# The first attention of an eight-part network: who scales the probabilities, and how heads of 96 fill tiles of 128

## What is computed

```python
q = (latents @ Wq.T).reshape(b, q_len, H, HD)        # H, HD = 16, 96; latents: layernorm of x
k = (hidden @ Wk.T).reshape(b, s_len, KV, HD)        # KV = 4; hidden: context (64 rows), then latents (256)
v = (hidden @ Wv.T).reshape(b, s_len, KV, HD)
q = q.transpose(0, 2, 1, 3).reshape(b, KV, G, q_len, HD)      # G = 4 heads for one of keys
scores = jnp.einsum('bkgqd,bksd->bkgqs', q, k) * scale        # scale = 96 ** -0.5; 320 keys
attn = jax.nn.softmax(scores.astype(jnp.float32), axis=-1)
out = jnp.einsum('bkgqs,bksd->bkgqd', attn, v)
return out.transpose(...).reshape(b, q_len, H * HD) @ Wo.T
```

## Time and profile before

| | us |
|---|---|
| runs, median (lowest to highest) | 1707.35 (1707.07 to 1708.24) |
| profiled execution, its own time | 1711.2 |
| its span, first to last instruction | 1709.4 |
| mean granted clock of TensorE in it, as a share of 2.4 GHz | 0.893 |

### The profile page before, as it was taken

How to read it: one execution, slowest core, us unless ns; L and a number is a source line. 1 busy time by engine, 2 the same in 40 slices (tenths; PEclk the granted TensorE clock), 3 DMA queues, 4 the chain that set the end, 5 groups by cost and what they waited for, 6 DMA issues and landing times.

```text
span 1709.4 us, 18898 instructions
## 1 busy us (share of the span) xinstructions
PE 1443.9 (84%) x6489; PEld 1131.2 (66%) x6489; DVE 1083.9 (63%) x2489; ACT 458.6 (27%) x994; POOL 296.5 (17%) x170
## 2 busy tenths in 40 slices
PE   6569999998999898899646878858999778789998
PEld 5347776776677667688545767747887546567786
DVE  4556876767777666948886756554446399944142
ACT  3223423332343333313131202101221333322010
POOL 4101111111111111202021002111543121012120
PEclk9779999999999999999855699557999889899999
DMA  5521232322232212222001112200112000001011
GB/s 184 159 77 46 80 82 68 82 74 58 64 89 71 75 50 69 72 66 67 25 26 46 42 40 60 63 18 1 50 49 62 26 25 1 1 27 60 16 36 49
DMA packets 99407, 96.40 MB, mean 56 GB/s; under 512 B 13138, under 2 KB 72418, under 8 KB 99314
## 3 DMA queue, kind: packets, MB, share of 16 engines
q1 hardware_dynamic: 98802, 94.35, 19.0%
q0 software_dynamic: 512, 0.85, 0.2%
HBM read 84.34 MB, written 10.82 MB: 56 GB/s over the span
## 4 chain that ended last, share of the span: by engine, by line
PE 62%; DVE 25%; issue 4%; ACT 4%; DMA 2%; SPq 1%; POOL 1%; DVEq 0%; ACTq 0%; POOLq 0%
PE bank L1636 48%; PE bank L1977 5%; PE bank L1728 4%; DVE nf_y L1581 3%; DVE st L1141 2%; DVE xn L1159 1%; PE bank L1661 1%; DVE xT L1118 1%; PE bank L1718 1%; DVE mx L1192 1%; DVE mx L1498 1%; ACT e L936 1%; DMA nf_w<-in_L_w 1%; DVE sm L1510 1%; SPq L767 1%
## 5 line engine op out<-in xcount | busy, mean ns | idle before, releaser
L1636 PE MATMUL bank<-xT,slots 128*128 128x512 f32 (+1 forms) x1920 | 467.6, 402 | 9.6 <-DVE xT L1118 7.8
L1636 PEld LDWEIGHTS bank<-xT,slots 128*128 128x128 f32 (+1 forms) x1920 | 354.8, 186 | 109.0 <-issue 8.9
L813 POOL TENSOR_TENSOR slots<-staging,slots 128x1024 fp32r<-128x1024 f32 (+4 forms) x97 | 230.5, 2379 | 1103.0 <-ACT slots L903 1103.0
L1581 DVE TENSOR_SCALAR nf_y<-nf_w 128x512 fp32r<-128x512 f32 (+2 forms) x495 | 232.2, 496 | 29.0 <-PE bank L1977 28.0
L1636 PE MATMUL bank<-slots,h 128*128 128x512 f32 (+1 forms) x728 | 178.8, 405 | 20.1 <-DVE h L1248 13.9
L1977 PE MATMUL bank<-nf_y,nf_d 128*128 128x512 f32 (+2 forms) x495 | 170.6, 429 | 10.3 <-DVE nf_y L1581 8.0
L1636 PEld LDWEIGHTS bank<-slots,h 128*128 128x128 f32 (+1 forms) x728 | 140.8, 194 | 56.1 <-DVE h L1248 14.8
L903 ACT ACTIVATE slots<-staging 128x1024 fp32r<-128x1024 f32 (+4 forms) x97 | 98.1, 1018 | 189.9 <-PE bank L1636 174.2
L936 ACT ACTIVATE e<-bank,mx 128x320 f32<-128x320 f32 x128 | 66.4, 523 | 271.1 <-DVE mx L1195 254.0
L1977 PEld LDWEIGHTS bank<-nf_y,nf_d 128*128 128x128 f32 (+1 forms) x495 | 95.3, 197 | 47.0 <-issue 15.5
L1214 DVE TENSOR_TENSOR x<-bank,x 128x512 f32<-128x512 f32 x72 | 49.7, 690 | 110.9 <-PE bank L1636 110.6
(11 more groups left out here) (246 smaller groups left out, 1897.8 us busy)
## 6 DMA issues: line engine op xcount, KB each, us to landing
staging<-in_L_wqkT SPq DMA_DIRECT2D x16, 480.0 KB, 3.8
nf_out<-nf_w SPq DMA_DIRECT2D x30, 256.0 KB, 2.1
staging<-nf_out SPq DMA_DIRECT2D x30, 256.0 KB, 2.8
staging<-in_L_woT SPq DMA_DIRECT2D x16, 384.0 KB, 3.5
staging<-in_L_w SPq DMA_DIRECT2D x12, 512.0 KB, 4.0
nf_a<-nf_max SPq DMA_DIRECT2D x40, 128.0 KB, 3.6
nf_r<-nf_rcp SPq DMA_DIRECT2D x40, 128.0 KB, 3.4
nf_w<-in_L_w SPq DMA_DIRECT2D x15, 256.0 KB, 4.4
```

The costliest lines, as they stand in the source:

```text
L813: g.tensor_tensor(lo, split_source(i), hi.bitcast(FP32), ALU.subtract).then_inc(*sig.mark("weight_low", i))
L1581: v.tensor_scalar(nf_y[0:rows, i % STAIR_RING, 0:size], w_, bound, first, compare, ALU.mult)\
L1636: ins = mm(dst, l_, r_, start=i == 0, stop=i == len(passes) - 1)
```

## The change

It has three parts.

1. **Probabilities.** The reciprocals stay on VectorE; the two multiplications of 128x320 go to ScalarE, as copies with a factor from SBUF for each row. In the list they keep the place of `scale0(n-1)`, so ScalarE does them after the exponentials of unit n and before the copies of `turn0(n-2)`.
2. **The factor of the scores** is multiplied into the queries when they are evicted (both parts), so that the exponential needs no scale and the small multiplication of the maxima goes.
3. **Four heads in three tiles.** The host lays out the query weights of a group as three tiles of 128 columns: 96 of head j and 32 of head 3. `q0` gets 128 partitions. Each of the three products is evicted by two instructions, of 96 and of 32 partitions, the second to the place of head 3 in the fourth plane of `q0`. The output of head 3 is evicted in three pieces of 32 partitions, each to the upper 32 partitions of one of the three planes, so that `o0` multiplies three full tiles of 128 rows, with rows of the output weights in the same order. The chunks of `o0` are then 128 partitions with two tiles and with one.

The planner's cost of a `q0` step goes from 2.6 to 3.5.

```diff
-    steps += [("k0", 0), ("kc0", 0)] + [("q0", 0, h) for h in range(HPG)]
+    steps += [("k0", 0), ("kc0", 0)] + [("q0", 0, j) for j in range(QT0)]
...
-                steps += [("q0", s + 1, h) for h in ((0, 1), (2,), (3,))[j - 5]]
+                steps.append(("q0", s + 1, j - 5))
...
-        q0 = sb("q0", [HD0, 2, 2, HPG, HALF], F32R, s0)
+        q0 = sb("q0", [P, 2, 2, HPG, HALF], F32R, s0)
...
-            for i in range(2):
-                rows = a["L0_woT"][(s % G0 * HPG + 2 * i) * HD0:(s % G0 * HPG + 2 * i + 2) * HD0]
-                chunk(("o0", s, i), HD0, (2, D), [((slice(None),), rows.rearrange("(h p) n -> p h n", p=HD0))])
+            for i, n in enumerate((2, 1)):
+                rows = a["L0_woT"][(s % G0 * QT0 + 2 * i) * P:(s % G0 * QT0 + 2 * i + n) * P]
+                chunk(("o0", s, i), P, (n, D), [((slice(None),), rows.rearrange("(h p) n -> p h n", p=P))])
...
ScalarE:
-            def q0_(s, h):
-                high("q0", (s, h), q0[:, s % 2, 0, h], psum(("q0", s, h))[0:HD0])
+            def q0_(s, j):
+                bank = psum(("q0", s, j))
+                act.wait_ge(*sig.when("q0_product", (s, j)))
+                sc.activation(q0[0:HD0, s % 2, 0, j], bank[0:HD0], ACT.Copy, scale=HD0 ** -0.5)
+                sc.activation(q0[spare(j), s % 2, 0, QT0], bank[HD0:P], ACT.Copy, scale=HD0 ** -0.5).then_inc(*sig.mark("q0_high", (s, j)))
...
+            def scale0(n):
+                act.wait_ge(*sig.when("sums0", n))
+                for i in range(TPB):
+                    e = e0[:, (2 * n + i) % E0_RING]
+                    sc.activation(e, e, ACT.Copy, scale=sm[:, n % 4, 2 + i:3 + i]).then_inc(*sig.mark("probs0", (n, i)))
...
             def pv0(n, s, bl, h):
-                high("pv0", n, q0[:, s % 2, 0, h, bl * S:(bl + 1) * S], psum(("pv0", n))[0:HD0, 0:S])
+                cs, bank = slice(bl * S, (bl + 1) * S), psum(("pv0", n))
+                if h < QT0:
+                    high("pv0", n, q0[0:HD0, s % 2, 0, h, cs], bank[0:HD0, 0:S])
+                    return
+                act.wait_ge(*sig.when("pv0_product", n))
+                for j in range(QT0):
+                    ins = sc.activation(q0[HD0:P, s % 2, 0, j, cs], bank[spare(j), 0:S], ACT.Copy)
+                ins.then_inc(*sig.mark("pv0_high", n))
...
VectorE (its q0_ and pv0 change in the same way: two and three subtractions for one):
             def scores0(n, s, bl, h):
...
-                link(ins)
-                v.tensor_scalar(mx[:, n % 4, 2:4], mx[:, n % 4, 0:2], HD0 ** -0.5, None, ALU.mult)\
-                    .then_inc(*sig.mark("max0", n))
+                ins.then_inc(*sig.mark("max0", n))
 
             def scale0(n):
                 dve.wait_ge(*sig.when("exp0", (n, TPB - 1)))
-                link(v.reciprocal(sm[:, n % 4, 2:4], sm[:, n % 4, 0:2]))
-                for i in range(TPB):
-                    v.tensor_scalar(e0[:, (2 * n + i) % E0_RING], e0[:, (2 * n + i) % E0_RING], sm[:, n % 4, 2 + i:3 + i], None, ALU.mult)\
-                        .then_inc(*sig.mark("probs0", (n, i)))
+                v.reciprocal(sm[:, n % 4, 2:4], sm[:, n % 4, 0:2]).then_inc(*sig.mark("sums0", n))
...
TensorE:
-                qk(s, ("q0_product", (s, h)), h * HD0, (h + 1) * HD0, lambda k: xt(k, hf * HALF, (hf + 1) * HALF), bank[0:HD0])
+                qk(s, ("q0_product", (s, j)), j * P, (j + 1) * P, lambda k: xt(k, hf * HALF, (hf + 1) * HALF), bank[:])
...
-                pe.wait_ge(*sig.when("q0_low", (s, h)))
+                pe.wait_ge(*sig.when("q0_low", (s, min(h, QT0 - 1))))
...
-                pairs = [([q0[:, s % 2, p, h, i * P:(i + 1) * P] for p in range(2)], [w[h // 2][p][:, h % 2] for p in range(2)])
-                         for h in range(HPG)]
+                pairs = [([q0[:, s % 2, p, j, i * P:(i + 1) * P] for p in range(2)], [w[j // 2][p][:, j % 2] for p in range(2)])
+                         for j in range(QT0)]
```

45 lines of the change are left out of this document (32 added, 13 removed).

## The result

The changed kernel takes 1743.84 us (median of 4 runs, 1741.22 to 1747.87) against 1707.80 for the kernel before beside it. The ratio is 1.0212, 95% interval 1.0188 to 1.0237: 36 us slower, where 34 us faster was forecast. The profiled execution of the changed kernel has 1741.5 us.

A forecast was written before the change was run, and what follows sets the result against it. TensorE, 94% busy, was taken to pace the first attention from 130 to 620 us. Profiled 1711.2 - 40.3 + 5 + 1 = 1677 us, so 1673 us for the median of runs; range 1652 to 1697.

The forecast's parts named there:

- +5: First attention's new instruction order: 14 us back at seven stage starts, 9 off for the removed multiplication; bounds -19 and +30.
- the chain stays hidden: Units with a projection: TensorE needs 4.13 + 2.9 us, the ScalarE-VectorE chain 5.0, so the longer chain costs nothing there.
- The 2 us of room: Units with a projection: slack between TensorE's 4.13 + 2.9 us and the chain's 5.0, used as argument against ScalarE's queue.
- 14 for them and for head 3's evictions together: Two bare units at each stage start: longer chain makes TensorE wait 2 us, seven times, 14 us back.
- rival 3: Slower: ScalarE's queue becomes the path, scalings ahead of the turned copies; 64 + 19 less 40 gives +43, 1750 us; chance 0.06.
- -40.3: First attention: removed matmuls worth their 0.24 us spacing; output products 23.0 us, query products of stages 2 to 7 17.3.
- The outputs' 23.0 us: o0 products in the first attention: 8 stages x 12 fewer matmuls x 0.24 us, 23.0 us off.
- The queries' 17.3: q0 products of stages 2 to 7, where TensorE is full: 6 x 12 fewer matmuls x 0.24 us, 17.3 us off.
- The bound of +30: Worst case for the new order: all 3.0 us lost at each stage start, and TensorE's clock lower a while after each.
- a clock under 0.95: Sign of a wrong forecast: TensorE's granted clock in the first attention's stretch below 0.95, against 0.98 before.
- forecast -9: Stage starts: the multiplication between maximum and exponential, held up by GpSimd's splits, falls away; 9 us off.
- The tail: After the last unit, of head 3, o0 waits for three evictions in series instead of one: 1 us more, unhidden.

The follow-up runs named there:

- e5: Kernel before with only the scores' factor moved into the query evictions and the small multiplication of the maxima gone: 1704.82 us, ratio 0.9967.
- e7: Kernel before with the factor in the evictions and only the outputs packed; queries unpacked, scalings on VectorE, query cost 2.6: 1690.59 us, ratio 0.9894.
- e13: e3 with the planner's cost of a query product 10.4/3 for 3.5, so a stage sums as in the kernel before: 1693.14 us, ratio 0.9910.
- e3: Changed kernel with the scaling of the probabilities back on VectorE; factor and packing stay: 1703.31 us, ratio 0.9969.
- e1: Kernel before with only the scaling of the probabilities moved to ScalarE: 1740.01 us, ratio 1.0187.
- e16: e7 with two unused 32x320 copies a unit added on ScalarE at the scalings' place; VectorE keeps its scalings: 1722.49 us, ratio 1.0082.
- e9: e3 with planner's costs that put every step but the fourth query product where the kernel before has it: 1715.42 us, ratio 1.0032.
- e11: e9 without the second evictions of the query tiles from stage 2 on, so head 3 uses old queries: 1690.81 us, ratio 0.9880.
- e10: e7 with two query products a stage evicted twice, on ScalarE and VectorE, and no matmul removed: 1705.58 us, ratio 0.9980.
- e15: e7 without two of head 3's three output evictions from stage 2 on: 1688.47 us, ratio 0.9880.
- e17: Kernel before with the planner's cost of a query product 2.625 for 2.6, so a stage sums to 10.5: 1714.99 us, ratio 1.0043.
- e18: Changed kernel with the planner's cost of a query product 10.4/3 for 3.5: 1737.55 us, ratio 1.0168.

## Why the prediction was wrong

From the kernel before to the changed one in the parts that the runs had, by their ratios times 1708 us: factor -5.6 (e5), packed outputs -12.5 (e7), packed queries with even costs +2.7 (e13, with an interval that takes in 0), the planner's cost +10 (e3), the scalings on ScalarE +41 (changed kernel). The sum is +36, as it has to be for steps in a row; in another order a step is worth something else, as the scalings' 32, 41 and 44 us show. TensorE over the attention, from 56 us on, in us:

| | length | busy | idle | at 1.2 GHz |
|---|---|---|---|---|
| before | 580.6 | 518.6 | 62.0 | 65 |
| changed | 603.9 | 508.4 | 95.4 | 120 |
| e1, scaling alone | 606.2 | 535.9 | 70.3 | 99 |
| e3, scaling back | 564.6 | 489.7 | 74.9 | 92 |
| e7, outputs packed | 558.6 | 495.6 | 63.0 | 58 |
| e13, even costs | 559.0 | 483.6 | 75.3 | 72 |
| e16, two copies added to e7 | 585.9 | 509.3 | 76.6 | 82 |

**Right, with their sizes.** 192 matmuls fewer. The spacing of matmuls with 96 and with 128 rows: twelve took 3.05 us, nine 2.34; less the last one's 0.40 that is 0.241 and 0.243 us. The scaling on ScalarE takes 0.555 us a piece (forecast 0.52) and a pair 1.01. The evictions cost as whole ones, by length and not by partitions:

```profile
L953 ACT ACTIVATE e<-e,sm 128x320 f32<-128x320 f32 x108 | 54.4, 555 | 4.5 <-DVE sm L1226 4.4
...
L937 ACT ACTIVATE q<-bank 96x512 fp32r<-96x512 f32 x20 | 11.9, 593 | 2.9 <-PE bank L1666 2.9
L938 ACT ACTIVATE q<-bank 32x512 fp32r<-32x512 f32 x20 | 11.8, 592 | 0.2
```

The Trainium skill's formula (ScalarE: Activation LUTs) gave 0.546 as an estimate; the trace has 0.555. Its rule to put a multiplication on VectorE was right here. The reason that the runs show lies in the queue, more than in the single instruction (0.555 us against VectorE's 0.384).

**The step that failed first: "+5" for the new order**, with "in the units with a projection beside them (2.9 us more of TensorE) the chain stays hidden". The 2 us of room came from a unit of 5.0 us with *one* background step on VectorE. The trace of before had the real number:

```profile
L1581 DVE TENSOR_SCALAR nf_y<-nf_w 128x512 fp32r<-128x512 f32 x317 | 158.2, 522 | 10.6 <-PE bank L1977 9.9
```

That is 317 steps for the stretch's 57 units, 2.8 us a unit where I had counted 0.42. The list of steps puts 2 or 3 of them into each of the two bare units of a stage, and in most stages 5 to 9 into each of the six others, the very ones with a projection. TensorE's longer work there left VectorE little room: 38.6 us of waits for TensorE in the stretch, 0.7 us a unit in the mean and not 2. That the background steps took the room is argued from these counts; no run took them away. I said of VectorE "neither is the bound by its sum", from busy time alone. So a longer chain counts in far more units than the two bare ones: the scalings cost 32 to 44 us where I had 14 for them and for head 3's evictions together, and e16 gives 32 us for 64 pairs, 0.5 us of each pair's 0.9. That was rival 3's mechanism. Its +43 stands near the result's +36 in part by luck: it took 64 us for the scalings, 19 for head 3 and -40 for the matmuls, where the runs have 32 to 44, 2 to 6 and some -12, and it had nothing for the planner's 10. I gave it 0.06, on the strength of that room.

**The second: "-40.3", matmuls worth their spacing.** The view behind it was TensorE busy for 94% of the stretch. That tells what a matmul costs if all else follows. The outputs' 23.0 us brought 12.5: against e5 TensorE is busy 21 us less and idle 7 us more. The queries' 17.3 brought nothing: with even costs e13 is as fast as e7 within the intervals (TensorE busy 12 us less and idle 12 more), and in e9's order they bring nothing even without the evictions (e11). They stood in units where VectorE had 5 to 8 background steps, and the eviction that came with each was nearly as dear as the matmuls saved (e10: 15 us for 16). What they would bring in the even order without their evictions is open.

**The third: the clock, counted at nothing.** The bound of +30 named it, the sum had no term for it, and one of the forecast's own signs of being wrong was a clock under 0.95: it is 0.93. The matmuls that stay take 36 us longer in the attention, about 27 of it by the estimate above.

**The rest.** The factor: forecast -9, measured -5.6 alone and -15 where the queue is tighter. The blocks of L1195 did pass to a background step, but that isn't free: at 212.52 us three of them took 2.83 us beside a split of GpSimd (2.22 us from 212.17), 1.6 more than three of 0.42, with the next maxima behind them. The trace agrees here too with the shared port of the Trainium skill (SBUF — State Buffer, SBUF: two separate sides). Head 3's evictions: 14 us of the forecast's working hung on them and on the pair at the stage starts; e15, which leaves out two evictions of three from stage 2 on, finds 2 to 6. The tail: TensorE waits 2.33 us before the last `o0` where it waited 0.70, so +1.6 for +1. "The planner's new cost leaves the background work where it was": it moved few steps, and they cost 7 us (e17, e18) to 10 (e13).

**What beats both kernels**: factor and packed outputs (e7), 1.06% faster than the kernel before [0.88%, 1.25%]; with packed queries and the cost of 10.4/3 too (e13), 0.90%.

## What to carry to other kernels

For an engine that works in order, busy time says little of the room it has, and busy time plus waits says nothing. Ask for whom it waits: the waits for the engine that sets the pace are its room, here 0.7 us a unit against a pair of 1.0, and a unit's background work belongs into the count of its chain. Find the loop that goes through several queues and ask of every moved instruction whether it lies on it: here, taking 0.8 us off one member of the loop and putting 1.0 on another gained little and cost 32 to 44 us. Give short waits of TensorE a price in its clock too. After changing the number of steps that a planner counts, look at where it puts the others, and try the change with the old sums and an even split.

## What was unexpected of the hardware

A copy of 32 partitions by 320 columns that nobody waits for takes 458 ns on ScalarE, and 128 of them cost 25 to 32 us, though ScalarE is busy for only 49% of the stretch (239.11 of 490 us). And waits of TensorE that are short and spread over the stretch go with a lower clock: from 130 to 620 us the changed kernel has 44 of them, 3 over 3 us and none over 3.8, TensorE is busy for 89% of the time (434.95 of 490), and yet it has 14 spells at 1.2 GHz, 70 us in all, and a granted clock of 0.93 for 0.98.
